# Q and K of 21 pairs of heads as seven block products, with kept sums of weights and sums of y

## What is computed

```python
q = (x @ Wq).reshape(Bsz, seq, H, DK).transpose(0, 2, 1, 3)
k = (x @ Wk).reshape(Bsz, seq, H, DK).transpose(0, 2, 1, 3)
v = (x @ Wv).reshape(Bsz, seq, H, DV).transpose(0, 2, 1, 3)
def step(carry, seg):
    mem, z = carry
    qq, kk, vv = seg
    sigma_q = jax.nn.elu(qq) + 1.0
    scores = jnp.einsum('bhsk,bhtk->bhst', qq, kk) / scale
    att_dot = jax.nn.softmax(scores, axis=-1) @ vv
    att_mem = sigma_q @ mem / (sigma_q @ z)
    sigma_k = jax.nn.elu(kk) + 1.0
    delta = vv - sigma_k @ mem / (sigma_k @ z)
    ...
    out = att.reshape(Bsz, SEG, H * DV) @ Wo
```

## Time and profile before

| what | value |
|---|---|
| runs | 1582.48, 1583.34, 1584.22 us; median 1583.34 |
| profiled execution: its span | 1581.4 us |
| the same execution's own time | not listed apart; the runs lie 1.1 to 2.8 us above the span, which is what lies around it |
| PE, DVE, ACT, POOL busy | 98%, 77%, 49%, 39% of the span |
| DMA moved | 262.04 MB, mean 166 GB/s |

### The profile page before, as it was taken

One profiled execution on the slowest core, in us unless ns is written; L12 is line 12 of the kernel. 1 busy time (PEld: TensorE's weight loads), 2 busy tenths in 40 slices (PEclk: granted clock), 3 DMA queues, 4 the chain that ended last, 5 costly groups with the idle time before them and its releaser, 6 DMA issues.

```text
span 1581.4 us, 26868 instructions
## 1 busy us (share of the span) xinstructions
PE 1547.0 (98%) x9574; PEld 1377.9 (87%) x9574; DVE 1219.7 (77%) x2719; ACT 782.1 (49%) x1687; POOL 615.2 (39%) x433
## 2 busy tenths in 40 slices
PE   4899999999999999999999999999999999999999
PEld 2699989999999999998999999989888888888887
DVE  8889888787878888778775773665897888687785
ACT  3576566445535626535546552653554443344442
POOL 3666585322222222222001000134664465666662
PEclk9999999999999999999999999999999999999999
DMA  5375685595473485474467547348211222311111
GB/s 177 124 246 191 223 292 195 180 392 184 161 276 127 154 286 201 147 254 160 174 228 280 210 171 283 110 141 279 88 54 54 60 89 72 107 46 62 54 41 54
DMA packets 109381, 262.04 MB, mean 166 GB/s; under 512 B 11200, under 2 KB 36160, under 8 KB 107840
## 3 DMA queue, kind: packets, MB, share of 16 engines
q1 hardware_dynamic: 90384, 227.28, 40.5%
q10 hardware_dynamic: 18864, 33.04, 6.5%
HBM read 212.03 MB, written 48.25 MB: 165 GB/s over the span
## 4 chain that ended last, share of the span: by engine, by line
PE 90%; DVE 6%; issue 2%; DMA 1%; ACT 1%; POOL 0%; SPq 0%; ACTq 0%; DVEq 0%
PE psG L595 17%; PE psG L597 17%; PE psG L596 17%; PE psX L771 4%; PE psX L726 3%; PE psX L595 3%; PE psX L597 3%; PE psX L596 3%; PE psZ L752 3%; PE psZ L743 3%; PE psZ L751 2%; PE psZ L597 2%; PE psY L597 2%; PE psY L596 2%; PE psZ L596 2%
## 5 line engine op out<-in xcount | busy, mean ns | idle before, releaser
L2076 POOL TENSOR_TENSOR wl<-stage,wh 128x512 fp32r<-128x512 f32 x160 | 233.5, 1481 | 147.4 <-ACT wh L1597 144.7
L595 PE MATMUL psG<-yh,wh 128*128 128x512 f32 x646 | 263.1, 407 | 0.0
L597 PE MATMUL psG<-yh,wl 128*128 128x512 f32 x646 | 253.0, 392 | 0.0
L596 PE MATMUL psG<-yl,wh 128*128 128x512 f32 x646 | 252.1, 390 | 0.0
L2144 POOL TENSOR_TENSOR vs<-v,omb 128x512 f32<-128x512 f32 x64 | 92.1, 1460 | 388.9 <-PE psX L726 216.0
L597 PEld LDWEIGHTS psG<-yh,wl 128*128 128x128 f32 x646 | 121.3, 188 | 26.8
L595 PE MATMUL psG<-wh,yh 128*128 128x256 f32 x480 | 141.6, 295 | 0.0
L595 PEld LDWEIGHTS psG<-yh,wh 128*128 128x128 f32 x646 | 121.9, 189 | 20.9 <-DVE sg L1274 0.3
L596 PEld LDWEIGHTS psG<-yl,wh 128*128 128x128 f32 x646 | 121.9, 189 | 20.5
L597 PE MATMUL psG<-wh,yl 128*128 128x256 f32 x480 | 135.7, 283 | 0.0
L596 PE MATMUL psG<-wl,yh 128*128 128x256 f32 x480 | 135.7, 283 | 0.0
(11 more groups left out here) (279 smaller groups left out, 4291.6 us busy)
## 6 DMA issues: line engine op xcount, KB each, us to landing
wh<-high_o SPq DMA_DIRECT2D x52, 512.0 KB, 3.6
wl<-low_o SPq DMA_DIRECT2D x52, 512.0 KB, 4.7
stage<-in_w SPq DMA_DIRECT2D x64, 256.0 KB, 3.1
wh<-high_k SPq DMA_DIRECT2D x23, 512.0 KB, 3.7
wl<-low_k SPq DMA_DIRECT2D x23, 512.0 KB, 5.0
wh<-high_q SPq DMA_DIRECT2D x23, 512.0 KB, 4.1
wl<-low_q SPq DMA_DIRECT2D x23, 512.0 KB, 5.8
wh<-high_v SPq DMA_DIRECT2D x22, 512.0 KB, 4.0
```

The lines of the kernel that those rows point to most:

```text
L595: e.matmul(out, lh, rh, start=first, stop=False, skip_group_check=check)
L596: e.matmul(out, lh, rl, start=False, stop=False, skip_group_check=check)
L597: return e.matmul(out, ll, rh, start=False, stop=last, skip_group_check=check)
L2076: e.tensor_tensor(lo, raw, hi, ALU.subtract).then_inc(p_wl, 1)
```

## The change

The 21 pairs with n > 8 and n not a multiple of 8 (`FASTN`) get Q and K in another way. The matrix of 512 channels x 512 tokens y is cut into four blocks (halves of channels, halves of tokens); the weights of Q and K together are the other 2x2 matrix, with Q as one row of blocks and K as the other and the halves of channels as columns. A scheme of Strassen's kind makes the 2x2 block product with seven products in place of eight. Each product has 2 heads x 2 channel blocks x 3 = 12 matmuls of 256 columns.

PE's parts. Of pair nx, in a pair that is no burst: P1 in place of the first half of K head 0, P6 the second, P7 behind `pv`, P5 behind `update 2`, and P4, P2, P3 as the tail behind `recall 3`. In a burst, P1 stands ahead of the third quarter of Wo, P6 and P7 on both sides of the fourth, and P5, P4, P2, P3 behind `recall 3`. The start of a fast pair is turned round: first the scores by halves of tokens, then `turn_k`, then `turn_att`.

```diff
+            def product(n, which):
+
+
+                b, f = n // NG, FAST_NO[n]
+                chain, other, third = banks_of(n)
+                blocks = y_blocks(b)
+                piece = (OPERANDS["k"] + OPERANDS["q"])[which]
+                i = PIECE[piece[0], n, piece[1]]
+                if which == P1:
+                    bank, rhs, first, last = chain, blocks[11], True, True
+                    if is_burst(n - 1):
+                        w.wait_ge(a_pt, 2 * (n - 1) + 1)
+                    else:
+                        w.wait_ge(a_v, 2 * n - 1)
+                elif which == P6:
+                    bank, rhs, first, last = chain, (TH[:, 1], TL[:, 1]), False, True
+                    w.wait_ge(a_tk, 3 * f + 1)
+                elif which == P7:
+                    bank, rhs, first, last = chain, (TH[:, 2], TL[:, 2]), False, True
+                    w.wait_ge(a_tk, 3 * f + 2)
+                elif which == P4:
+                    bank, rhs, first, last = chain, (TH[:, 3], TL[:, 3]), False, True
+                    w.wait_ge(a_tk, 3 * f + 3)
+                elif which == P5:
+                    bank, rhs, first, last = other, (TH[:, 0], TL[:, 0]), True, True
+                    if is_burst(n - 1):
+                        w.wait_ge(a_pt, 2 * (n - 1) + 2)
+                    else:
+                        w.wait_ge(a_v, 2 * n)
+                elif which == P3:
+                    bank, rhs, first, last = other, blocks[22], False, True
+                    wait_summed(w, n, "k", 1)
+                else:
+                    bank, rhs, first, last = third, blocks[21], True, True
+                    if is_burst(n - 1):
+                        w.wait_ge(v_xb, 4 * ((n - 1) // 4 - 1) + 3)
+                    else:
+                        w.wait_ge(a_pt, 2 * (n - 1) + 1)
+                wait_split(w, i)
+                if which in (P5, P6, P7, P4):
+                    w.wait_ge(a_th, 4 * b)
+                    w.wait_ge(p_tl, 4 * b)
+                hi, lo = ring(i)
+                for j in range(2):
+                    for c in range(2):
+                        cols = slice(256 * c + 128 * j, 256 * c + 128 * j + 128)
+                        m = three(bank[:, 256 * j:256 * j + 256], hi[:, cols], lo[:, cols], rhs[0][:, c, :],
+                                  rhs[1][:, c, :], first and j == 0 and c == 0, last and j == 1 and c == 1, True)
+                m.then_inc(pe_p, 1)
...
+            def scores_by_halves(n):
+                for half in range(2):
+                    wait_summed(w, n, "k", half)
+                    wait_summed(w, n, "q", half)
+                    for j in range(2):
+                        w.wait_ge(v_jn, 8 * (n - 1) + 7 + j)
+                        for s in (2 * half, 2 * half + 1):
+                            m = e.matmul(X[j][:, seg(s)], qT[:, j, seg(s)], kT[:, j, seg(s)], start=True, stop=True)
+                        if half == 1:
+                            m.then_inc(pe_s, 1)
...
+                if n in FAST_NO:
+                    scores_by_halves(n)
+                    turn_k(n)
+                else:
+                    turn_k(n)
+                    scores(n)
+                fast = nx in FAST_NO
...
+                elif fast:
+                    product(nx, P6)
...
+                if burst and fast:
+                    product(nx, P1)
+                    wo(n // 4 - 1, 2)
+                elif burst:
                     wo(n // 4 - 1, 2)
                     wo(n // 4 - 1, 3)
+                elif fast:
+                    product(nx, P7)
                 elif more:
                     if n > 0:
                         kq_part(nx, "k", 1, 0)
@@ -880,13 +1104,25 @@
                     w.wait_ge(v_f3, 1)
                     up(0, 1, "3", G[1])
                 update(n, 2)
-                if burst:
+                if burst and fast:
+                    product(nx, P6)
+                    wo(n // 4 - 1, 3)
+                    product(nx, P7)
+                elif burst:
                     kq_part(nx, "k", 0, 0)
                     kq_part(nx, "k", 0, 1)
+                elif fast:
+                    product(nx, P5)
                 elif more:
                     kq_part(nx, "q", 0, 0)
                 recall(n, 3)
-                if burst:
+                if fast:
+                    if burst:
+                        product(nx, P5)
+                    product(nx, P4)
+                    product(nx, P2)
+                    product(nx, P3)
```

DVE adds the other sums to what ACT copied; sigma(k) and sigma(q) go by halves of tokens in place of heads:

```diff
+            def add_sum(n, kind, half):
+
+
+                f = FAST_NO[n]
+                chain, other, third = banks_of(n)
+                dst, bank, taken, made = {("k", 1): (kT, other, 3, P5), ("q", 0): (qT, third, 1, P2),
+                                          ("q", 1): (qT, other, 2, P3)}[kind, half]
+                w.wait_ge(a_tk, 3 * f + taken)
+                w.wait_ge(pe_p, PRODUCTS * f + made + 1)
+                cut = dst[:, :, tokens(half)]
+                e.tensor_tensor(cut, by_heads(bank), cut, ALU.add).then_inc(v_cx, 1)
+
+            def sigma_of_half(n, kind, k):
+                src, dst = (kT, sk) if kind == "k" else (qT, sq)
+                half = half_of(kind, k)
+                wait_summed(w, n, kind, half)
+                w.wait_ge(a_ke if kind == "k" else a_qe, 2 * n + k + 1)
+                w.wait_ge(pe_am, 6 * (n - 1) + (4 if kind == "k" else 6))
+                w.wait_ge(pe_kt, 2 * n)
+                e.scalar_tensor_tensor(dst[:, :, tokens(half)], src[:, :, tokens(half)], 1.0, by_heads(etmp[k]), ALU.add,
+                                       ALU.max).then_inc(v_sk if kind == "k" else v_sq, 1)
...
+                if nx in FAST_NO:
+                    add_sum(nx, "k", 1)
                     sigma(nx, "k", 0)
-                if more:
+                    add_sum(nx, "q", 0)
+                    sigma(nx, "k", 1)
+                    add_sum(nx, "q", 1)
```

ACT: at the start of a fast pair; the copies; and behind step 6:

```diff
+                if n in FAST_NO:
+                    sigma_parts(n, "q", 1)
                 copy_kn(n)
                 if n == 0:
...
+            def take_sum(n, made):
+
+
+                f = FAST_NO[n]
+                chain, other, third = banks_of(n)
+                w.wait_ge(pe_p, PRODUCTS * f + made + 1)
+                w.wait_ge(pe_s, 2 * n)
+                if made in (P1, P6):
+                    w.wait_ge(v_sq, 2 * n)
+                    dst = qT[:, :, tokens(0 if made == P1 else 1)]
+                else:
+                    w.wait_ge(v_sk, 2 * n)
+                    dst = kT[:, :, tokens(1 if made == P7 else 0)]
+                e.activation(dst, by_heads(chain), ACT.Copy).then_inc(a_kc if made == P4 else a_tk, 1)
+
+            def sigma_parts(n, kind, k):
+
+                half = half_of(kind, k)
+                wait_summed(w, n, kind, half)
+                if kind == "k":
+                    w.wait_ge(v_sq, 2 * (n - 1) + k + 1)
+                else:
+                    w.wait_ge(v_sk, 2 * n + k + 1)
+                e.activation(by_heads(etmp[k]), (kT if kind == "k" else qT)[:, :, tokens(half)], ACT.Relu,
+                             scale=-1.0).then_inc(a_km if kind == "k" else a_qm, 1)
+                minus_exp(n, kind, k)
...
+                if fast:
+                    if burst:
+                        split_hi(here + 11)
+                        take_sum(nx, P7)
+                    sigma_parts(nx, "k", 0)
+                    take_sum(nx, P4)
+                    sigma_parts(nx, "k", 1)
+                    if nx + 1 not in MADE_S:
+                        split_hi(here + (14 if burst else 6))
+                    sigma_parts(nx, "q", 0)
+                elif burst:
```

POOL makes four sums of raw weights for each of the pairs 9 to 15 (`MADE_S`), which are split and kept like other tiles and loaded back in later batches, and, at the end of each of the batches 0 to 2, four sums of blocks of y in ten operations, split a pair later:

```diff
+            def sums_of_weights_of(n):
+
+
+                at = [PIECE["s", n, x] for x in (1, 2, 3, 4)]
+                k1, q0, k0, q1 = (staged(i)[:, :] for i in at)
+                k = 4 * (n - MADE_S[0])
+                for i in at[:3]:
+                    wait_staged(w, i)
+                e.tensor_tensor(k1, k0, k1, ALU.add).then_inc(p_ss, 1)
+                w.wait_ge(p_ss, k + 1)
+                e.tensor_tensor(k0, q0, k0, ALU.subtract).then_inc(p_ss, 1)
+                w.wait_ge(p_ss, k + 2)
+                e.tensor_tensor(q0, k1, q0, ALU.subtract).then_inc(p_ss, 1)
+                w.wait_ge(p_ss, k + 3)
+                wait_staged(w, at[3])
+                e.tensor_tensor(q1, q1, q0, ALU.subtract).then_inc(p_ss, 1)
```

The ring is cut anew. A slot is now 512 KB: high and low part of one half (a piece) side by side. K takes four pieces, Q three (`OPERANDS`), V two, a tile of Wo two. The order of the stream is as before. There are 9 slots in the attention and 11 in the feed-forward part:

```diff
-NRING = 6
+NRING = 9
+NRING_FFN = 11
...
+FASTN = [n for n in range(NG + 1, NN) if n % NG]
+FAST_NO = {n: f for f, n in enumerate(FASTN)}
+MADE_S = range(NG + 1, 2 * NG)
+PRODUCTS = 7
+P1, P6, P7, P5, P4, P2, P3 = range(PRODUCTS)
+OPERANDS = {"k": (("q", 0), ("s", 2), ("s", 3), ("s", 1)), "q": (("k", 1), ("q", 1), ("s", 4))}
+SUM_ORDER = (1, 3, 2, 4)
+RAW_OF = {1: ("k", 1), 2: ("q", 0), 3: ("k", 0), 4: ("q", 1)}
```

(6 more changed lines are left out.)

572 lines of the change are left out of this document (380 added, 192 removed).

## The result

The changed kernel takes **1779.5 us** (median of 4 runs, 1769.8 to 1782.1) against 1583.1: ratio 1.123, 95% interval 1.120 to 1.126. It is slower, as forecast, but by 196 us and not by 33, and far outside the range. The profiled execution has a span of 1780.3, so it is the longest of the four.

The account below looks back on a forecast made before the run. PE was taken as the bound, busy 98% of the span with no slack to absorb waits. Terms -23 + 33 + 3 + 18 + 2 = +33 on 1583 gave 1616 us, slower, range 1574 to 1640.

Parts of the forecast that it names:

- 2.2 us a pair: End of 15 fast pairs prepared without burst: PE waits for DVE's sums and ACT's key copies, 33 us in all.
- a gain of 1.1 us a pair: Q and K products: 84 narrow matmuls replace 48 wide ones, ends 0.9 and 1.2, -23 us over 21 pairs.
- narrow matmuls would cost 1.9 us a pair more: Opposing estimate from the skill's figures, about 98 ns at 256 columns; the prediction set it aside for the profile's rows.
- The wait for DVE's second sum: Scores of a fast pair: second half could start at 5.1 but waits for Q's second sum until 6.95.
- the ring of the feed-forward part: nothing: Feed-forward part with its smaller ring: PE's work unchanged, loads covered by a pair or more of lead, cost nothing.
- if PE waits in the feed-forward part: One of the listed signs that would show the prediction wrong: PE waiting in the feed-forward part.
- The wait is 3.0 us ... +18 ... over 6 bursts: Bursts: P1 waits for the load of Q's first piece, whose slot frees late; +18 us, 0 to 23.
- The following pieces fall on slots freed a product or a quarter ahead; hidden: Bursts: loads of pieces after Q's first get their slots early enough, so they cost nothing.
- POOL has room ... +2: Pairs 9 to 15: POOL's new sums and splits fit, slowing DVE 0.3 us for 7 pairs; +2, up to 8.
- Rival 3: Pairs 9 to 15: DVE becomes the bound as POOL's 12 us collide with it; 1641 us, chance 0.11.
- In the 6 bursts ... the sums come in time ... 0.5: Bursts: four products follow `recall 3`, leaving mostly `turn_att`'s 0.5 us wait for key copies; +3, 0 to 6.
- The term of ACT's copies: ACT's copies: four of 0.6 us in place of four, as many as before, hidden.

Follow-up runs that it names:

- run 3: Changed kernel with DVE doing the last sum of queries before the second maximum of keys instead of behind it: 1767.8 us.
- run 12: run 4 with DVE's three sums of products in each fast pair cut to one column of 256, the rest left out of the computation: 1661.4 us.
- run 1: Changed kernel with a twelfth slot for weight pieces in the feed-forward part: 1710.2 us.
- run 2: Changed kernel with product P1 issued behind the third quarter of Wo in bursts instead of ahead of it: 1746.7 us.
- run 13: Changed kernel with seven edits already in, plus P1's load in pair 8 issued ahead of the three raw blocks: 1643.7 us.
- run 5: run 4 with SP loading pair 9's fourth raw block, in pair 8, ahead of the eight stores of Wo pieces: 1667.7 us.
- run 8: run 4 with the two loads for the first modulation issued at the start of pair 24: 1668.7 us.
- run 17: Changed kernel with ten edits already in, plus POOL's order in bursts altered and P6 waiting only for its own low sum of y: 1626.3 us.
- run 10: run 4 with less room for DVE's scans in the last stretch of bursts 8 to 20 and more in three middle stretches: 1661.0 us.
- run 9: Kernel before the change, with 2 to 12 unneeded DVE reciprocals ahead of the maxima of five pairs, so PE idles: 1614.8 us.
- runs 7: run 4 with ACT doing the last exponential of queries and the key copies ahead of the scans' exponentials at burst ends: 1673.3 us.
- run 6: run 4 with POOL's four sums of raw weights in pairs 9 to 15 cut to one column of 512, the rest left out: 1665.8 us.
- run 4: Changed kernel with the edits of run 1, run 2 and run 3 together: 1676.5 us.

## Why the prediction was wrong

**The sign was right, and the local price where nothing else is late.** The term "2.2 us a pair" less "a gain of 1.1 us a pair" says 1.1 longer; pairs 25, 26, 27 and 29 are 1.11 longer. It held in these and in pair 22, five of the 15; the others lost 1.6 to 8.7. The matmuls: 12 of a product run from 994.31 to 995.75, 0.120 each, so 84 cost 10.1 us, and the gain is 0.9, the low end given. The figures of the Trainium skill (TensorE: Matmul & The Clock Gate, section Back-to-back issue gap), from which the prediction estimated that narrow matmuls would cost 1.9 us a pair more, do not hold here: 0.120 at 256 columns against 0.229 at 512, as the earlier trace rows said. The wait for DVE's second sum was placed right too: swapping it with the maximum gave 0.73 a pair (run 3), and shortening the sums another 0.5 (run 12).

**"... the ring of the feed-forward part: nothing ... a whole pair or more of lead covers the loads": 64 us (run 1).** This is the step that failed by most. I counted the lead of the loads and not who waits for the slot. The slot is waited for by ACT's split, in order, ahead of the sigmoids. The slot arithmetic that I did for Q's first piece, done for w3, would have shown it: the piece 11 before it belongs to a w2 that PE has not read yet. The prediction had "if PE waits in the feed-forward part" among its signs of being wrong, and that sign came.

**"The wait is 3.0 us ... +18 ... over 6 bursts": mis-sized.** Bursts 16, 20 and 28 gave waits of 2.9, 3.5 and 3.5, as worked out. Pair 8 gave 13.9, pair 12 5.9, pair 24 5.4: all six 35.0, and 33 us came back (run 2). My sum took the load's landing time from a burst without raw loads. At pair 8, SP's raw loads wait for POOL, and P1's load waits with them (in run 13 it went ahead of them and P1's wait was gone); for pairs 12 and 24 the cause was not taken apart. By the Trainium skill (DMA: Bandwidth & Descriptors, section Anatomy of one DMA) 512 KB take an estimated 3.2 us; its figures are for DMAs that GpSimd issues, and SP issues these. The page of the changed kernel has a median of 5.9 for the 46 loads of `kept_q`, so the error went the other way.

**"The following pieces fall on slots freed a product or a quarter ahead; hidden": wrong for P6 and P7.** In pair 8 P6 waited 8.5 us, in pair 12 5.8, in pair 24 P7 5.1. Three different engines' orders did it, and each was tested: SP's stores ahead of a raw block (run 5, 9 us), ACT's sigmoids waiting for the modulation's loads (run 8, 8 us), POOL's low pieces (run 17, 15 us).

**"POOL has room ... +2": mis-sized.** It has room over a pair, but its new work of the batch's start stands in the same burst as the raw Wo tiles, ahead of a piece that PE wants. Rival 3 had POOL's collision with DVE as the mechanism; what run 17 gave back came from POOL's own order. No run prices the collision.

**"In the 6 bursts ... the sums come in time ... 0.5": wrong for the pair behind the burst.** DVE ends a burst with three more sums and then over 5 us of scans ahead of the next pair's maxima. PE's waits there were 0.9 to 4.5 us; run 10 gave 15 us back.

**What no term held: the clock.** All waits of the forecast were priced at their own length. Of the 199 us that the span grew, 52 are PE's busy time, at a lower granted clock. Run 9 shows the price by itself: 1.4 to 2.8 us for each gap from 3.6 to 8.2. The term of ACT's copies ("hidden") was not quite nothing either: 6.3 us in run 17.

## What to carry to other kernels

When a change deepens what a step takes from a ring, work out for every piece whose slot it falls on, and then name the engine that waits for that slot and what stands behind it in its order; the loads' lead is not the answer. On a full PE, an edit worth 1 us a pair must be asked first what each in-order queue (SP, ACT, DVE, POOL) has ahead of its new inputs in the busiest stretch, not in the average one. When taking away a wait moves it to another engine, as in runs 7 and 13, look for the engine without idle time there before the next edit.

## What I had not expected of the hardware

- A gap of PE of 1.0 us left the clock alone; gaps of 3.6 to 8.2 us were followed by matmuls at half the granted clock, 1.2 GHz, with 1.4 to 2.8 us lost beyond the gap. It does not grow with the gap: 8.2 us cost less than 4.8, because the clock had fallen while PE still stood idle (run 9).
- Taking part of a gap away can give back the clock behind it as well: in run 6 PE's idle time in pair 13 fell by 3.2 us and its busy time by 2.1, at a clock of 1.00 in place of 0.90, so the pair became 5.3 us shorter.
- A load behind large stores was slow: in pair 8 of run 4 a raw block of 256 KB was issued at 335.87 behind eight stores of 512 KB, and POOL, idle for 10.17 us, got it at 342.95, 7.1 us later; such a load has a median of 3.0 on the page of the changed kernel. This is one case; that the stores are the cause is argued from it and from run 5, where the load went ahead of them and P6's gap fell by 7.9 us.
